# Four-layer graph attention: twelve instead of ten groups of two heads mixed while the adjacency is packed, with three, two or no tiles beside each

## The chip, the cores and the metric

The kernel runs on one core of one Trainium2 chip. The metric is the device time of one execution in microseconds (us); the time quoted for a kernel is the median of its runs. Engines are named as the profile names them: PE is TensorE (PEld its weight loads), DVE is VectorE, ACT is ScalarE, POOL is GpSimd and SP is SyncE, whose queue issues the transfers spoken of here.

## What is computed

Four graph-attention layers over 4096 nodes with 256 features, each followed by a residual sum and a layer norm. The change touches the first layer alone, which has four heads of 64 features:

```python
h = jnp.einsum('nf,hfd->hnd', x, W)
s_src = jnp.einsum('hnd,hd->hn', h, a1)
s_dst = jnp.einsum('hnd,hd->hn', h, a2)
e = jax.nn.leaky_relu(s_src[:, :, None] + s_dst[:, None, :], 0.01)
e = jnp.where(adj[None, :, :] == 0, -jnp.inf, e)
alpha = jax.nn.softmax(e, axis=-1)
out = jnp.einsum('hij,hjd->hid', alpha, h)
```

`adj` is a 4096 x 4096 int32 matrix, 64 MB, and it is used by all four layers. It is read once, at the start, and kept on the chip as one bit per entry.

## The kernel before, in words

**Packing.** The adjacency comes in 32 tiles of 128 rows. A tile is two halves of 1 MB (`load_adj`, L416, on SP's queue). There is room for one tile, one buffer for each half, so the transfer of a half is issued only when DVE has converted the same half of the tile before it. `convert` (L1712, the instruction is L1717) makes a half into bf16; `pack_half` (L1307, L1313) multiplies it on PE by powers of two so that eight entries become one byte; ACT stores the finished tile (`store_packed`, L935, L938). Seven tiles are packed before the attention begins (`PACKED_FIRST`), the other 25 beside its first groups.

**Mixing.** Each head is one pass, and a pass is eight groups of 512 target nodes. A group has eight units; in one unit ACT makes four tiles `above` (L967), DVE makes two masks from them and from the packed bits (L1792, L1797, L1800), and PE multiplies the masks by the head's values: 32 matmuls (L1370, L1373). Two sets of masks are kept, so DVE is at most two units ahead of PE. In the units 1 to 4 of the next group DVE adds up the banks (`sum_parts`, L1951); then POOL divides (`quotient`, L615: five instructions from L626 to L639), and this must have ended two groups later, when DVE wants the same slot of sums (`banks_ready`, L1953). A group needs the four tiles of its own 512 nodes packed.

**The opening.** `FRONT` (L70) lists the groups that run while tiles are still being packed, as pairs of head and group; its places are counted from 0 here. It holds all eight groups of head 0, with two of head 1 between them. Beside the group at place `at` stand the tiles `packs_of(at)`, three for each place until they are used up: three each at places 0 to 7, one at place 8, none at place 9. DVE converts one half in each of the units 0 to 5, right behind the masks of the unit; PE packs a half one unit later; ACT stores a tile behind `above` of units 4 and 6, the third one behind unit 0 of the next group.

**SP's queue.** For each place SP issues the loads of the tiles of the place before it, then waits until ACT has ended `above` of the group before it (`s_above`, L456), then loads the next row of scores (L432), and goes on with the next place. So the first tile of a place is asked for when ACT has ended the last unit of the group ahead of it, behind the row.

**Values of the next heads.** POOL also makes the values of each later head, eight calls of `values_of` (L654) with twelve instructions each (L542 to L556). Those of head 1 are made at places 0 to 2. Those of head 2 take the room of head 0's values, so they wait for the last group of head 0 (L669, `s_unit`), which is place 9, the end of `FRONT`. PE starts the pass of head 2 only when all eight are there (`one_pass`, L1393, `s_vals`). After `FRONT` the six other groups of head 1 follow, which are called places 10 to 15 here; the pass of head 2 begins at place 16. `front` (L660) sets POOL's order: the first values, the quotient of place 9, two more values, and from then on one call of `values_of` and one quotient in turn.

Of the kernel before, what the change touches and what calls it, by code (L numbers as in the profile page):

```python
# [21 lines left out]
T = N // P  # L22
# [10 lines left out]
BITS = 8  # L33
# [33 lines left out]

FRONT = [(0, 0), (0, 1), (0, 2), (0, 3), (1, 0), (0, 4), (0, 5), (0, 6), (1, 1), (0, 7)]  # L70
PACKS = 3


def packed_before(at):

    return min(PACKED_FIRST + at * PACKS, T)


def packs_of(at):

    return range(packed_before(at), packed_before(at + 1))


assert all(packed_before(at) >= (g + 1) * GT for at, (p, g) in enumerate(FRONT))

AHEAD = 3
# [78 lines left out]
def gnn_kernel(nc, A, out, last_layer=3):  # L168

    with ExitStack() as ctx:  # L170
# [406 lines left out]
        def _(pool):  # L577
# [82 lines left out]
            def front():  # L660

                values = {0: (0, 1, 2), 1: (3, 4, 5), 2: (6, 7)}
                for at, (p, g) in enumerate(FRONT[:-1]):
                    for v in values.get(at, ()):
                        values_of(0, 1, v)
                    if at == 0:
                        pool.wait_ge(s_rowexp, 1)
                    quotient(0, p, g, at % 2, at)
                pool.wait_ge(s_unit, len(FRONT) * BITS + CREDIT)  # L669
                values_of(0, 2, 0)  # L670
                quotient(0, *FRONT[-1], 1, len(FRONT) - 1)
                values_of(0, 2, 1)
                values_of(0, 2, 2)
                for g in range(2, NG):
                    if g + 1 < NG:
                        values_of(0, 2, g + 1)
                    quotient(0, 1, g, g % 2)
                chain.settle()
# [179 lines left out]
        def _(act):  # L858
# [68 lines left out]
            def stores_behind(at, par, k):  # L927

                other = GT * (1 - par)
                if k in (4, 6) and k // 2 - 2 < len(packs_of(at)):  # L930
                    store_packed(packs_of(at)[k // 2 - 2], other + k // 2 - 2)
                if k == 0 and at > 0 and len(packs_of(at - 1)) == PACKS:
                    store_packed(packs_of(at - 1)[PACKS - 1], GT * par + PACKS - 1)

# [75 lines left out]
            def attention(l):  # L1010

                act.wait_ge(s_kpass, l * H + 1)
                if l == 0:
                    for at, (p, g) in enumerate(FRONT):
                        group(0, p, None, at % 2, first=(at == 0), at=at)
                        if at == 0:
                            scores_of(0, 1)
                else:
                    for par in range(2):
                        group(l, 0, 0, par, first=(par == 0))  # L1020
                    with act.Fori(1, NG // 2) as gg:
                        for par in range(2):
                            group(l, 0, gg, par)
                for p in range(1, H):
                    if l > 0 or p > 1:
                        scores_of(l, p)
                    if l == 0 and p == H - 1:
                        for g in range(NG):
                            group(l, p, g // 2, g % 2, elu=ELU_AT.get(g))
                        continue  # L1030
                    with act.Fori(1 if l == 0 and p == 1 else 0, NG // 2) as gg:
                        for par in range(2):
                            group(l, p, gg, par)

# [239 lines left out]
        def _(pe):  # L1274
# [81 lines left out]
            def group(l, slot, par, at, packs=(), first=False):  # L1356

                for k in range(BITS):
                    if first and k % 2 == 0:
                        pe.wait_ge(s_vfirst, first_values_before(l) + k + 2)  # L1360
                    pe.wait_ge(s_sides, at * BITS + (TURN[l] * H * UNITS + k + 1 + CREDIT))
                    pe.nop(nofuse=True)
                    for q in range(Q):
                        v = values[:, slot, k * Q + q, :]
                        start, final = (k == 0 and q == 0), (k == BITS - 1 and q == Q - 1)
                        for it in range(GT):
                            acc = bank[GT * par + it]
                            rows = slice(it * P, (it + 1) * P)
                            if l < 3:
                                pe.matmul(acc[:, 0:KW], pos[:, k % 2, q, :].bitcast(FP8)[:, rows], v[:, 0:KW],  # L1370
                                          start=start, stop=final, skip_group_check=True)

                                last = pe.matmul(acc[:, KW:2 * KW], neg[:, k % 2, q, :].bitcast(FP8)[:, rows],  # L1373
                                                 v[:, KW:2 * KW], start=False, stop=final, skip_group_check=True)
                            else:
                                last = pe.matmul(acc[:, 0:2 * KW], edge[:, k % 2, q, :].bitcast(FP8)[:, rows], v,  # L1376
                                                 start=start, stop=final)
                    last.then_inc(s_unit, 1)
                    if 1 <= k <= 2 * len(packs):
                        n, half = divmod(k - 1, 2)  # L1380
                        if half == 0:
                            if at == 0:
                                pe.wait_ge(s_src, 1)
                                pe.wait_ge(s_packed, PACKED_FIRST + CREDIT)
                            else:
                                pe.wait_ge(s_banksum, PACKS * (at - 1) + n + 1)
                        pack_half(packs[n], half, GT * (1 - par) + n)

            def one_pass(l, p):

                begun = p == 0 or (l == 0 and p == 1)
                if p > 0:
                    pe.wait_ge(s_vals, p * NG + values_before(l))  # L1393
                if p == 0:
# [1 line left out]
                        pe.wait_ge(s_sums, TURN[l] * SUMS + par + 1)  # L1396
                        group(l, 0, par, par, first=(par == 0))
                final = l == 3 and p == PASSES[3] - 1
                with pe.Fori(1 if begun else 0, NG // 2 - final) as gg:
                    for par in range(2):  # L1400

                        pe.wait_ge(s_sums, gg * 2 + (p * NG + TURN[l] * SUMS + par + 1))
                        pe.nop(nofuse=True)
                        group(l, p % 2, par, gg * 2 + (p * NG + par))
# [275 lines left out]
        def _(dve):  # L1680
# [313 lines left out]
            def group(l, g, gg, par, banks_before, norm=None, first=False, front=None, fold=None, ahead=None,  # L1994
# [7 lines left out]
                for k in range(BITS):  # L2002
# [53 lines left out]
                    if front is not None:  # L2056
                        if l == 0 and first and k == 0:
                            store_packed(PACKED_WOVEN + 1, 6 + (PACKED_WOVEN + 1) % 2)
                        if k < 2 * len(packs_of(g)):
                            convert(packs_of(g)[k // 2], k % 2)  # L2060
                    if fold is not None and k >= GT:
                        fold_weights(fold, k - GT)
                    if norm is not None:
# [17 lines left out]
            def attention(l):  # L2081
                if l == 0:
                    for at, (p, g) in enumerate(FRONT):
                        group(0, at, None, at % 2, 1 - at % 2 if at else None, first=(at == 0), front=g,
                              fold=1 if at == len(FRONT) - 1 else None)
                    one_pass(0, 1, 1)
                    one_pass(0, 2)
                    final_pass(0)
                    return
# [365 lines left out]
```

## Time and profile before

| | |
|---|---|
| median of 3 runs | 3026.6 us (3025.57 to 3028.38) |
| span of the profiled execution | 3025.2 us |
| PE busy | 2947.3 us, 97% of the span |
| DVE, ACT, POOL busy | 2138.8, 1921.5, 1173.2 us |
| HBM read | 97.73 MB, of which `adj` is 64 transfers of 1024 KB |

The span runs from the first to the last instruction of the profiled execution; it lies 1.4 us under the median of the runs. Idle time of PE counts directly, since PE is the engine that is busy nearly all the time; idle time of the others counts only where PE waits for them. A line such as L1370 is a line of the kernel before. Matmuls overlap, so their single durations (246 ns) are longer than the step from one to the next.

### The profile page before, as it was taken

To read this page: it belongs to the slowest core of one execution; us is meant where nothing else is said; L and a number is where in the kernel's file an instruction comes from. 1 tells how busy PE (TensorE), PEld (TensorE's weight loads), DVE (VectorE), ACT (ScalarE), POOL (GpSimd) and SP (SyncE) were. 2 spreads that over 40 slices of the span, in tenths; PEclk is the share of its full clock that TensorE was granted. 3 is DMA by queue.
4 is the path that set the end of the run, shared out by engine and by line. 5 is a ranking of instruction groups with operands and counts; after the bars stand their busy time and mean duration, and the time that the engine had idled before them with its cause. 6 is when DMAs were issued, how large, how long until landed. Compare 5 with 4: busy or idle time off the path is not lost.

```text
span 3025.2 us, 65221 instructions
## 1 busy us (share of the span) xinstructions
PE 2947.3 (97%) x24628; PEld 2580.8 (85%) x24628; DVE 2138.8 (71%) x3855; ACT 1921.5 (64%) x3414; POOL 1173.2 (39%) x1559
## 2 busy tenths in 40 slices
PE   7899999999989999999999999999999999989999
PEld 6899999999989999999998877888788878755555
DVE  5998888888988888888886556665666666562245
ACT  4777899999988999999995544454455444430000
POOL 0661385642226656564222023233333333444222
PEclk9999999999999999999999999999999999999999
DMA  8667100000100000000010000000000000000001
GB/s 289 203 206 246 60 15 11 14 11 15 61 12 15 11 11 14 11 14 11 15 34 12 4 1 4 4 1 4 1 4 4 1 1 1 2 1 1 0 14 42
DMA packets 41912, 104.55 MB, mean 35 GB/s; under 512 B 9856, under 2 KB 23424, under 8 KB 33536
## 3 DMA queue, kind: packets, MB, share of 16 engines
q1 hardware_dynamic: 39616, 101.61, 10.3%
q8 instruction: 111, 1.82, 0.2%
q10 hardware_dynamic: 2112, 0.52, 0.1%
q14 instruction: 73, 0.60, 0.1%
HBM read 97.73 MB, written 4.39 MB: 34 GB/s over the span
## 4 chain that ended last, share of the span: by engine, by line
PE 88%; DVE 5%; DMA 3%; ACT 2%; issue 2%; POOL 1%; SPq 0%; DVEq 0%; POOLq 0%; ACTq 0%
PE bank L1373 21%; PE bank L1370 21%; PE bank L1428 15%; PE bank L1466 13%; PE bank L1376 11%; DMA arena<-in_adj_dram 3%; PE bank L1301 2%; PE bank L1455 2%; PE bank L1442 1%; DVE rings L1797 1%; DVE arena L1717 1%; ACT above L967 1%; PE bank L1313 1%; PE bank L1351 1%; DVE rings L1792 1%
## 5 line engine op out<-in xcount | busy, mean ns | idle before, releaser
L1370 PE MATMUL bank<-values,rings 128*128 128x195 bf16 x8192 | 1413.3, 246 | 35.9 <-DVE rings L1800 24.0
L1373 PE MATMUL bank<-values,rings 128*128 128x195 bf16 x8192 | 1413.4, 249 | 0.0
L967 ACT ACTIVATE above<-srow,kpass 128x512 fp8e4<-128x512 f32 x2032 | 1280.1, 709 | 121.3 <-DVE rings L1800 114.6
L1370 PEld LDWEIGHTS bank<-values,rings 128*128 128x128 fp8e4 x8192 | 806.1, 98 | 45.1 <-issue 43.1
L1373 PEld LDWEIGHTS bank<-values,rings 128*128 128x128 fp8e4 x8192 | 788.7, 96 | 0.4
L1797 DVE TENSOR_TENSOR rings<-rings,above 128x512 uint32<-128x512 uint32 x512 | 399.6, 781 | 184.6 <-PE bank L1373 160.9
L1055 ACT ACTIVATE values<-srow,cmul 128x512 f32<-128x512 f32 x256 | 205.8, 814 | 411.2 <-PE bank L1466 410.3
L1800 DVE TENSOR_TENSOR rings<-rings 128x512 uint32<-128x512 uint32 x512 | 430.6, 841 | 17.3
L1466 PE MATMUL bank<-hv,values 128*128 128x257 f32 x1792 | 420.6, 380 | 0.0
L1466 PEld LDWEIGHTS bank<-hv,values 128*128 128x128 f32 x1792 | 335.0, 190 | 69.9 <-issue 25.2
L1376 PE MATMUL bank<-values,rings 128*128 128x390 bf16 x1920 | 320.4, 329 | 11.5 <-DVE values L1833 11.5
L1376 PEld LDWEIGHTS bank<-values,rings 128*128 128x128 fp8e4 x1920 | 186.8, 97 | 145.1 <-issue 14.5
L626 POOL TENSOR_TENSOR quot<-sums,cmul 128x260 f32<-128x260 f32 x64 | 50.3, 786 | 597.8 <-DVE sums L1951 475.9
L1792 DVE TENSOR_SCALAR rings<-packed 128x512 uint32 (+1 forms) x512 | 242.4, 474 | 5.8 <-ACT packed L938 5.7
L1907 DVE SCALAR_TENSOR_TENSOR values<-values,cmul,rings 128x512 f32<-128x512 f32 x256 | 192.0, 757 | 35.0 <-ACT values L1055 34.3
L759 POOL TENSOR_SCALAR zrow<-zrow 128x1 f32<-128x1 f32 x128 | 46.2, 361 | 429.4 <-DVE zrow L2159 429.3
L2022 DVE TENSOR_SCALAR rings<-packed 128x512 uint32 (+1 forms) x120 | 54.7, 456 | 201.0 <-PE bank L1376 200.9
L1951 DVE TENSOR_REDUCE sums<-bank 128x130 f32<-128x390 f32 x320 | 176.6, 554 | 3.7 <-PE bank L1351 2.0
L1428 PE MATMUL bank<-arena,above 128*128 128x256 f32 (+1 forms) x496 | 165.9, 482 | 0.8 <-ACT above L1110 0.8
L1428 PEld LDWEIGHTS bank<-arena,above 128*128 128x128 f32 x496 | 94.0, 190 | 53.1 <-issue 43.8
L1428 PE MATMUL bank<-quot,arena 128*128 128x256 f32 x512 | 118.3, 379 | 0.0
L762 POOL TENSOR_TENSOR zrow<-zrow,exponents 128x1 f32<-128x1 f32 x128 | 103.6, 809 | 19.6 <-POOL zrow L759 0.6
(223 smaller groups left out, 3482.9 us busy)
## 6 DMA issues: line engine op xcount, KB each, us to landing
arena<-in_adj_dram SPq DMA_DIRECT2D x64, 1024.0 KB, 5.0
srow<-src_dram SPq DMA_DIRECT2D x69, 256.0 KB, 3.1
x<-in_x_dram SPq DMA_DIRECT2D x4, 1024.0 KB, 11.4
out_dram<-x SPq DMA_DIRECT2D x7, 512.0 KB, 2.9
arena<-in_L_gnn_fe_w_dram SPq DMA_DIRECT2D x2, 512.0 KB, 6.9
arena<-in_L_gnn_W_hz_dram SPq DMA_DIRECT2D x1, 1024.0 KB, 7.6
arena<-in_L_gnn_g_w_dram SPq DMA_DIRECT2D x1, 1024.0 KB, 10.9
weights<-in_L_gnn_W_dram SPq DMA_DIRECT2D x3, 256.0 KB, 4.0
```

The source lines that it names most:

```text
L967: last = act.activation(above[:, k % 2, q, :], srow[:, par, :], ACT.Relu, scale=BIG, bias=kpass[:, p % 2, k * Q + q:k * Q + q + 1], satura ...
L1055: act.activation(w2[:, m % DEPTH, :], srow[:, g % 2, :], ACT.Relu, scale=b_col[:, jt:jt + 1], bias=c_neg[:, jt:jt + 1]).then_inc(E.relu, 1)
L1370: pe.matmul(acc[:, 0:KW], pos[:, k % 2, q, :].bitcast(FP8)[:, rows], v[:, 0:KW], start=start, stop=final, skip_group_check=True)
L1373: last = pe.matmul(acc[:, KW:2 * KW], neg[:, k % 2, q, :].bitcast(FP8)[:, rows], v[:, KW:2 * KW], start=False, stop=final, skip_group_chec ...
L1376: last = pe.matmul(acc[:, 0:2 * KW], edge[:, k % 2, q, :].bitcast(FP8)[:, rows], v, start=start, stop=final)
L1428: last = pe.matmul(dst, lhsT[k], rhs[k], start=(k == 0), stop=(k == len(lhsT) - 1))
L1466: last = pe.matmul(bank[it][:, 0:VW], w2[:, m % DEPTH, it * P:(it + 1) * P], hv[:, k * Q + q, :], start=(k == 0 and q == 0), stop=False)
L1792: dve.tensor_scalar(edge[:, r], words, shift[0], ONE, shift[1], ALU.bitwise_and).then_inc(s_dve, 1)
L1797: dve.tensor_tensor(pos[:, r], edge[:, r], above[:, r].bitcast(U32), ALU.bitwise_and).then_inc(s_dve, 1)
L1800: dve.tensor_tensor(neg[:, r], edge[:, r], pos[:, r], ALU.bitwise_xor).then_inc(s_sides, 1)
L1907: dve.scalar_tensor_tensor(out=w2[:, m % DEPTH, :], in0=w2[:, m % DEPTH, :], scalar=c_pos[:, jt:jt + 1], in1=edge[:, unit % 2, q, :].bitca ...
L1951: return dve.tensor_reduce(sums[:, slot, it, :, :], parts, AX.X, ALU.add)
```

## The change

Head 1 has four groups in the opening instead of two, so `FRONT` has twelve places. The last group of head 0 stands at place 10, and the last place, 11, is a group of head 1. The tiles beside the places are listed in a table: three at places 0 to 4 as before, then two at places 5 to 9, none at places 10 and 11. Where two tiles stand beside a group, DVE converts halves in units 0, 1, 3 and 4, and ACT stores them behind units 4 and 7. On POOL the first values of head 2 wait for place 10, then comes the quotient of place 11, then four calls of `values_of` in a row (`BEGUN` is 4) instead of two, then the turns from group 4 on. The loops over the rest of head 1 begin at group 4.

```diff
-FRONT = [(0, 0), (0, 1), (0, 2), (0, 3), (1, 0), (0, 4), (0, 5), (0, 6), (1, 1), (0, 7)]
+FRONT = [(0, 0), (0, 1), (0, 2), (0, 3), (1, 0), (0, 4), (1, 1), (0, 5), (1, 2), (0, 6), (0, 7), (1, 3)]
 PACKS = 3
+GROUP_PACKS = (3, 3, 3, 3, 3, 2, 2, 2, 2, 2, 0, 0)
+HALF_AT = {3: {0: (0, 0), 1: (0, 1), 2: (1, 0), 3: (1, 1), 4: (2, 0), 5: (2, 1)},
+           2: {0: (0, 0), 1: (0, 1), 3: (1, 0), 4: (1, 1)}, 0: {}}
+STORE_AT = {3: {4: 0, 6: 1}, 2: {4: 0, 7: 1}, 0: {}}
 def packed_before(at):
-    return min(PACKED_FIRST + at * PACKS, T)
+    return PACKED_FIRST + sum(GROUP_PACKS[:at])
+BEGUN = len(FRONT) - NG
...
-                pool.wait_ge(s_unit, len(FRONT) * BITS + CREDIT)
+                pool.wait_ge(s_unit, (FRONT.index((0, NG - 1)) + 1) * BITS + CREDIT)
                 values_of(0, 2, 0)
                 quotient(0, *FRONT[-1], 1, len(FRONT) - 1)
-                values_of(0, 2, 1)
-                values_of(0, 2, 2)
-                for g in range(2, NG):
+                for v in range(1, BEGUN + 1):
+                    values_of(0, 2, v)
+                for g in range(BEGUN, NG):
                     if g + 1 < NG:
                         values_of(0, 2, g + 1)
                     quotient(0, 1, g, g % 2)
...
-                if k in (4, 6) and k // 2 - 2 < len(packs_of(at)):
-                    store_packed(packs_of(at)[k // 2 - 2], other + k // 2 - 2)
+                if k in STORE_AT[GROUP_PACKS[at]]:
+                    n = STORE_AT[GROUP_PACKS[at]][k]
+                    store_packed(packs_of(at)[n], other + n)
...
-                    if 1 <= k <= 2 * len(packs):
-                        n, half = divmod(k - 1, 2)
+                    if k - 1 in HALF_AT[len(packs)]:
+                        n, half = HALF_AT[len(packs)][k - 1]
...
-                        if k < 2 * len(packs_of(g)):
-                            convert(packs_of(g)[k // 2], k % 2)
+                        if k in HALF_AT[GROUP_PACKS[g]]:
+                            n, half = HALF_AT[GROUP_PACKS[g]][k]
+                            convert(packs_of(g)[n], half)
```

Lines of the changed kernel are about ten higher from `front` on. On DVE at place 5 (its second and third unit; L1717, after the change L1728, converts a half, L1951 or L1962 sums a bank, the other lines make masks), before:

```order
L1717 TENSOR_SCALAR arena<-arena 128x2048 [waits pack_matmul,adj_loaded1]
L1792 TENSOR_SCALAR rings<-packed 128x512
L1797 TENSOR_TENSOR rings<-rings,above 128x512 [waits unit_multiplied,above_made,dve_chain]
L1800 TENSOR_TENSOR rings<-rings 128x512 [waits dve_chain]
L1951 TENSOR_REDUCE sums<-bank 128x130
L1717 TENSOR_SCALAR arena<-arena 128x2048 [waits pack_matmul,adj_loaded0]
```

and after:

```order
L1728 TENSOR_SCALAR arena<-arena 128x2048 [waits pack_matmul,adj_loaded1]
L1803 TENSOR_SCALAR rings<-packed 128x512
L1808 TENSOR_TENSOR rings<-rings,above 128x512 [waits unit_multiplied,above_made,dve_chain]
L1811 TENSOR_TENSOR rings<-rings 128x512 [waits dve_chain]
L1962 TENSOR_REDUCE sums<-bank 128x130
L1803 TENSOR_SCALAR rings<-packed 128x512
```

Behind the third unit no half is converted any more; the next one stands behind the fourth unit. The first conversion of the group, behind its first unit, keeps its place.

On POOL, behind the quotient of the last place of `FRONT` and the next three sets of values (L542 to L556, after the change L552 to L566), before:

```order
L553 CAST values<-vtmp_pool 128x4x65 [waits pool_chain]
L556 TENSOR_TENSOR values<-vtmp_pool,values 128x4x65 [waits pool_chain]
L626 TENSOR_TENSOR quot<-sums,cmul 128x260 [waits quotients_made,sums_made]
L627 TENSOR_TENSOR quot<-sums,cmul 128x260
L631 TENSOR_TENSOR quot<-quot 128x260 [waits pool_chain]
L635 TENSOR_TENSOR quot<-quot,exponents 128x4 [waits pool_chain]
```

and after:

```order
L563 CAST values<-vtmp_pool 128x4x65 [waits pool_chain]
L566 TENSOR_TENSOR values<-vtmp_pool,values 128x4x65 [waits pool_chain]
L552 COPY vtmp_pool<-emul 128x4
L553 TENSOR_TENSOR vtmp_pool<-hv,emul 128x4x64
L557 CAST values<-vtmp_pool 128x4x65 [waits pool_chain]
L560 TENSOR_TENSOR vtmp_pool<-vtmp_pool,values 128x260 [waits pool_chain]
```

Where a quotient (L626 and on) stood, a fourth set of values follows, and a fifth behind it; the next quotient, that of place 12, stands behind both.

## Rows read from the trace of the kernel before

**Rows 1.** The page: busy us of each engine, and the chain that ended last.

```profile
PE 2947.3 (97%) x24628; PEld 2580.8 (85%) x24628; DVE 2138.8 (71%) x3855; ACT 1921.5 (64%) x3414; POOL 1173.2 (39%) x1559
PE 88%; DVE 5%; DMA 3%; ACT 2%; issue 2%; POOL 1%; SPq 0%; DVEq 0%; POOLq 0%; ACTq 0%
```

**Rows 2.** PE's waits from 60 to 700 us: in all, times, longest.

```profile
PE bank L1370 <- DVE rings L1800: 17.7, 21, 2.3
```

**Rows 3.** Stretches: length, busy us (instructions) of PE, PEld, DVE, ACT, POOL, then PEclk.

```profile
204.10:231.47 27.37, 27.37 (x355) 27.28 (x353) 23.47 (x34) 21.60 (x36) 5.45 (x5) 1.00 0.67 225
231.47:259.86 28.39, 27.58 (x354) 27.23 (x353) 24.01 (x34) 21.70 (x36) 5.45 (x5) 1.00 0.71 231
259.86:289.47 29.61, 27.74 (x354) 27.19 (x353) 24.09 (x34) 21.93 (x36) 5.45 (x5) 1.00 0.68 225
289.47:317.79 28.32, 27.58 (x352) 27.24 (x353) 25.47 (x36) 21.47 (x36) 5.46 (x5) 1.00 0.80 268
317.79:363.66 45.87, 45.87 (x546) 45.50 (x545) 36.58 (x65) 41.37 (x67) 9.18 (x10) 1.00 0.05 17
407.45:495.13 87.68, 87.68 (x1026) 87.48 (x1025) 75.64 (x113) 81.12 (x130) 55.61 (x74) 1.00 0.04 12
```

**Rows 4.** PE in order of time: start, us, instruction [idle before it <- releaser].

```profile
256.23 1.05 PE L1313 MATMUL bank<-powers,arena 128*128 128x128 bf16 x16
257.12 0.25 PE L1370 MATMUL bank<-values,rings 128*128 128x195 bf16 x1
...
264.52 0.24 PE L1370 MATMUL bank<-values,rings 128*128 128x195 bf16 x1 [1.76 <-DVE rings L1800]
```

**Rows 5.** DVE in order of time, around the first conversions at places 5, 6, 7.

```profile
231.97 1.23 DVE L1717 TENSOR_SCALAR arena<-arena 128x2048 bf16<-128x2048 int32 x1 [2.42 <-DMA arena<-in_adj_dram]
...
261.36 1.23 DVE L1717 TENSOR_SCALAR arena<-arena 128x2048 bf16<-128x2048 int32 x1 [3.41 <-DMA arena<-in_adj_dram]
...
289.91 1.23 DVE L1717 TENSOR_SCALAR arena<-arena 128x2048 bf16<-128x2048 int32 x1 [0.69 <-DMA arena<-in_adj_dram]
```

**Rows 6.** SP's queue in order of time: the rows of scores ahead of each tile.

```profile
224.62 0.33 SPq L432 DMA_DIRECT2D srow<-src_dram  x1
...
252.92 0.33 SPq L432 DMA_DIRECT2D srow<-src_dram  x1
...
282.31 0.33 SPq L432 DMA_DIRECT2D srow<-src_dram  x1
```

**Rows 7.** ACT in order of time at place 5, units 4 to 6.

```profile
242.59 0.60 ACT L938 ACTIVATE packed<-bank 128x512 uint8<-128x512 f32 x1 [1.55 <-PE bank L1313]
243.09 5.00 ACT L967 ACTIVATE above<-srow,kpass 128x512 fp8e4<-128x512 f32 x8
```

**Rows 8.** POOL in order of time: first and last instructions of values and quotients.

```profile
379.68 0.38 POOL L542 COPY vtmp_pool<-emul 128x4 f32<-128x4 f32 x1
...
408.00 1.07 POOL L626 TENSOR_TENSOR quot<-sums,cmul 128x260 f32<-128x260 f32 x1
...
413.16 0.39 POOL L542 COPY vtmp_pool<-emul 128x4 f32<-128x4 f32 x1
...
422.13 1.07 POOL L626 TENSOR_TENSOR quot<-sums,cmul 128x260 f32<-128x260 f32 x1
...
474.83 0.92 POOL L556 TENSOR_TENSOR values<-vtmp_pool,values 128x260 bf16<-128x260 f32 x1
...
487.72 0.67 POOL L639 TENSOR_TENSOR hv<-quot 128x256 f32<-128x256 f32 x1
```

**Rows 9.** Two stretches behind an idle PE; columns as in the stretches above.

```profile
91.95:95.36 3.41, 3.41 (x23) 3.17 (x22) 3.34 (x5) 2.24 (x4) 0.00 (x0) 0.50 0.00 0
887.25:894.08 6.83, 4.05 (x26) 3.74 (x27) 5.67 (x11) 6.67 (x12) 1.96 (x3) 0.50 0.53 116
```

**Rows 10.** PE in order of time: what it waited for before those two.

```profile
91.70 0.24 PE L1370 MATMUL bank<-values,rings 128*128 128x195 bf16 x1 [2.29 <-DVE rings L1800]
...
890.03 0.32 PE L1370 MATMUL bank<-values,rings 128*128 128x195 bf16 x1 [5.73 <-DVE values L1833]
```

More of the change, by code:

```diff
@@ L65 @@
 TURN = {0: 0, 1: 1, 3: 2}
-FRONT = [(0, 0), (0, 1), (0, 2), (0, 3), (1, 0), (0, 4), (0, 5), (0, 6), (1, 1), (0, 7)]
+FRONT = [(0, 0), (0, 1), (0, 2), (0, 3), (1, 0), (0, 4), (1, 1), (0, 5), (1, 2), (0, 6), (0, 7), (1, 3)]
 PACKS = 3
+GROUP_PACKS = (3, 3, 3, 3, 3, 2, 2, 2, 2, 2, 0, 0)
+HALF_AT = {3: {0: (0, 0), 1: (0, 1), 2: (1, 0), 3: (1, 1), 4: (2, 0), 5: (2, 1)},
+           2: {0: (0, 0), 1: (0, 1), 3: (1, 0), 4: (1, 1)}, 0: {}}
+STORE_AT = {3: {4: 0, 6: 1}, 2: {4: 0, 7: 1}, 0: {}}
 def packed_before(at):
-    return min(PACKED_FIRST + at * PACKS, T)
+    return PACKED_FIRST + sum(GROUP_PACKS[:at])
 def packs_of(at):
     return range(packed_before(at), packed_before(at + 1))
+assert packed_before(len(FRONT)) == T and sum(p for p, g in FRONT) == FRONT[-1][1] + 1
 assert all(packed_before(at) >= (g + 1) * GT for at, (p, g) in enumerate(FRONT))
+BEGUN = len(FRONT) - NG
 AHEAD = 3
@@ L1030, in attention @@
                         continue
-                    with act.Fori(1 if l == 0 and p == 1 else 0, NG // 2) as gg:
+                    with act.Fori(BEGUN // 2 if l == 0 and p == 1 else 0, NG // 2) as gg:
                         for par in range(2):
@@ L1389, in one_pass @@
             def one_pass(l, p):
-                begun = p == 0 or (l == 0 and p == 1)
+                begun = 1 if p == 0 else BEGUN // 2 if (l, p) == (0, 1) else 0
                 if p > 0:
@@ L1398, in one_pass @@
                 final = l == 3 and p == PASSES[3] - 1
-                with pe.Fori(1 if begun else 0, NG // 2 - final) as gg:
+                with pe.Fori(begun, NG // 2 - final) as gg:
                     for par in range(2):
@@ L2085, in attention @@
                               fold=1 if at == len(FRONT) - 1 else None)
-                    one_pass(0, 1, 1)
+                    one_pass(0, 1, BEGUN // 2)
                     one_pass(0, 2)
```

## The prediction

> **What bounds the kernel now.** I read the page first: PE is busy 97% of the span and holds 88% of the chain that ended last [rows 1], so only what moves PE moves the time. Then PE's waits in the first 700 us: masks of DVE that came late cost it 17.7 us in 21 waits, the longest 2.3 us [rows 2]. Places 0 to 4 of the opening stay as they are, so the question is how much of this lies from place 5 on. The stretches are cut at the first matmul of a group: place 4, 5, 6, 7, then places 8 and 9 together, then places 12 to 15 [rows 3]. Four groups without packing take 87.68 us, 21.92 each, or 2.74 per unit. A packed half is worth the step from its first matmul to the next unit's, 257.12 - 256.23 = 0.89 us [rows 4]. Three tiles make a group 21.92 + 6 x 0.89 = 27.26 us. Place 4 took 27.37, which is PE's own pace. Places 5, 6 and 7 took 28.39, 29.61 and 28.32, so 1.13, 2.35 and 1.06 too much, and places 8 and 9 took 45.87 against 2 x 21.92 + 2 x 0.89 = 45.62, so 0.25 too much [rows 3]. In all 4.79 us: more than that the opening from place 5 on can't give.
>
> Where it comes from is seen at place 6. PE stood idle for 1.76 us before its second unit, waiting for DVE [rows 4]; DVE itself had stood idle for 3.41 us before its first conversion, waiting for the adjacency [rows 5]. That half was asked for right behind the row of scores, when ACT had ended the group before: the row was issued at 252.92 and the conversion began at 261.36, a lag of 8.44 us; at places 5 and 7 it was 7.35 and 7.60 [rows 5, 6]. From the start of the conversion to PE's second unit it took 264.52 - 261.36 = 3.16 us, and that unit was due 2.74 us behind the start of the group. So PE is late by (issue of the row - start of the group) + lag + 0.42. With -6.85, -6.94 and -7.16 us in the bracket, this gives 0.92, 1.92 and 0.86 us at places 5, 6 and 7, 3.70 of the 4.79.
>
> **The change part by part.** *What PE computes* is the same: the same groups, the same 25 tiles, and a group of head 1 costs PE what one of head 0 costs. Nothing is removed; work moves.
>
> *Two tiles instead of three.* PE needs 21.92 + 4 x 0.89 = 25.48 us for such a group. The first conversion still stands behind the first unit, and its transfer is still asked for when ACT has ended the group before. So the bracket decides. In a group of two tiles ACT stores the first tile behind unit 4, and must wait for PE to pack its second half, as it waited 1.55 us for it in the group before the change [rows 7]. PE ends that half 2.74 + 2 x 3.63 = 10.00 us into the group; the store takes 0.50 (243.09 - 242.59), and three more units of `above` follow at about 2.45 us, half of the 5.00 us that eight of its instructions took, less their overlap [rows 7]. This is 17.9 us, with some 0.3 us for the hand-overs 18.2, and the group ends at 25.48: a bracket of -7.25, hardly better than -6.94. Behind such a group PE is late by 0.52, 0.77 or 1.61 us for the lags 7.35, 7.60 and 8.44. I take 7.60, the middle one. Place 5 follows a group of three tiles as before and keeps its 0.92; places 6 to 9 make 4 x 0.77 = 3.1; the 0.25 at the end, where DVE also folds weights, moves to place 11. In all 4.3 against 4.79: a gain of 0.5, between a gain of 1.5 and a loss of 2.9. The rest of DVE's excess goes, since units without a conversion leave it room.
>
> *The other order of the groups.* Place 10 needs all 32 tiles. The last is packed 20.0 us into place 9 and stored by ACT right behind its last unit; DVE needs it for the first masks of place 10, which can't be finished before PE has ended unit 6 of place 9, at 22.7. The store has 2 us of cover, so I count nothing.
>
> *POOL, the values of head 2.* Here the change has a price. The first set waits for place 10 and is hidden in places 11 and 12. Then the order has the quotient of place 11, whose sums DVE makes only in place 12. A quotient of this kind ended at 487.72 + 0.67 = 488.39, and the group before which its sums were made began at 495.13 - 21.92 = 473.21 [rows 3, 8]: 15.2 us into the group. Seven sets are queued behind it, and two quotients among them, those of places 12 and 13. Three sets in a row took 408.00 - 379.68 = 28.32, so 9.44 each; one behind a quotient took 422.13 - 413.16 = 8.97; a quotient took 413.16 - 408.00 = 5.16 [rows 8]. Five sets at 9.44, two at 8.97 and two quotients are 75.5 us, and the last set is there 90.7 us behind the start of place 12. The pass of head 2 is due after four groups, at 87.7. PE waits 3.0 us; with all sets at 8.97 it is 0.6, with all at 9.44 it is 3.9. Before the change the last set ended at 474.83 + 0.92 = 475.75, some 19 us ahead of the pass at 495.13 [rows 3, 8]; two places are lost to it, 43.8 us, and only part comes back by making sets closer together. The quotient of place 12 ends about 67.5 us behind the start of place 12, and DVE wants it at 65.8 + 2: just in time.
>
> *The clock.* After an idle time of 2.29 us PE's granted clock was 0.50 (1.2 GHz) for 3.41 us, and 23 PE instructions ran where 3.41 / 2.74 x 32 = 40 fit at the full clock: 17 lost, 1.4 us. After 5.73 us idle it was 0.50 for 6.83 us, of which PE worked 4.05, so 2.0 us lost [rows 9, 10]. After the 1.76 us at place 6 the clock stayed at 1.00 [rows 3, 4]. A wait of 3.0 us is nearest to the first: 1.4 us, between nothing and 2.0. The Trainium skill, "TensorE: Matmul & The Clock Gate", section "Terms", prices such a stretch at its whole length times the withheld share of the clock. By this the two stretches would cost 1.7 and 3.4 us; the sum would come to +4.2 or +5.9 instead of +3.9. The rows disagree for the longer one, since PE was idle in part of it anyway.
>
> The sum: -0.5 + 3.0 + 1.4 = +3.9 us. The profiled execution becomes 3025.2 + 3.9 = 3029.1, and with the 1.4 us by which the median of the runs lies above it, 3030.5.
>
> **The rivals.** *The values come in time.* If POOL makes each set in 8.97 us, PE waits 0.6 us and the clock holds: -0.5 + 0.6 = +0.1, 3026.7 us. For it speaks that sets behind a quotient were that short; against it that five of seven stand behind another set.
>
> *The transfers come in time.* If the lag at places 6 to 9 is 6.8 us or less, their 3.1 us go too: +0.8, 3027.4 us. DVE's evener work speaks for it; against it, that the three lags in the rows were all over 7.3 and that nothing in the change issues these transfers earlier against the end of the group.
>
> *The transfers come late, and the kernel is slower.* If each of the four lags is like the 8.44 at place 6, the loss of 2.9 takes the place of the gain: 2.9 + 3.0 + 1.4 = +7.3, 3033.9 us. There are now four such starts behind two-tile groups where there were two late ones, and each pays. It decides from a mean lag of about 8.2, where the sum passes 6.05 us.
>
> *The change does not do what it says.* It can't reach a gain of 6 us: all that is late from place 5 on is 4.79.
>
> **How the numbers follow.** 0.2% of 3026.6 is 6.05 us, about what a measurement of this kernel can tell from no change. The forecast, a late head 2 and a small gain in the opening (3028 to 3032.5), gets 0.60; values in time 0.15; transfers in time 0.07; transfers late 0.17; a gain over 6 us 0.01. So faster 0.01, same 0.82, slower 0.17. The range, 3026.5 to 3034.0, holds the forecast, the case of early transfers, half of the case of values in time and most of the late transfers.
>
> **What would show it.** Right: places 6 to 9 of about 26.2 us each, with DVE idle before the first conversion of each; POOL without a pause from some 15 us into place 12 until the last set; PE idle for about 3 us before the first matmul of place 16, waiting for POOL's `values`, and a stretch at 0.50 behind it. Wrong: places 6 to 9 at 25.5 us, or 27; no idle PE before place 16; or a wait at place 10 or 15 that I counted at nothing.

## The result, and the profile after

The changed kernel took 3036.99 us, the median of six runs (3033.65 to 3041.35). The kernel before took 3027.49 us in six runs beside them. The ratio is 1.0033, with a 95% interval from 1.0023 to 1.0043: a loss of 9.5 us. It is outside the range of the prediction, which ended at 3034.0. The profiled execution took 3038.3 us with a span of 3036.2, so the two profiles differ by 11.0 us of span. The parts below are those of these two profiles.

On the page, the busy time of each engine and the chain that ended last (as [rows 1]):

```profile
PE 2952.6 (97%) x24628; PEld 2584.7 (85%) x24628; DVE 2138.2 (70%) x3855; ACT 1920.3 (63%) x3414; POOL 1173.3 (39%) x1559
...
PE 83%; DVE 6%; POOL 3%; DMA 3%; issue 2%; ACT 2%; SPq 0%; POOLq 0%; DVEq 0%; ACTq 0%
```

PE holds 83% of the chain where it held 88%; DVE gained one point and POOL two. PE is busy 5.3 us longer with the same 24628 instructions. A slower clock does this: where its granted clock was 0.50 a matmul took 0.37 us (at 319.73), and at 1.00 it took 0.25, all of it counted as busy. Three such stretches are not in the profile before. One, in place 0, cost one unit 1.6 us and was made good by a shorter wait in place 1; the other two are at places 8 and 16, below.

The stretches from place 5 on, cut at the first matmul of each group (as [rows 3]: length, busy us (instructions) of PE, PEld, DVE, ACT, POOL, then PEclk). They are places 5, 6, 7, 8, 9, 10, 11, then 12 to 15 together, then place 16, the first group of head 2:

```profile
231.52:258.18 26.66, 25.63 (x323) 25.43 (x322) 21.83 (x32) 21.41 (x35) 5.15 (x5) 1.00 0.47 167
258.18:285.10 26.92, 25.64 (x323) 25.43 (x322) 21.83 (x32) 21.12 (x35) 5.15 (x5) 1.00 0.49 169
285.10:311.82 26.72, 25.62 (x322) 25.41 (x321) 21.83 (x32) 21.10 (x35) 5.15 (x5) 1.00 0.47 163
311.82:341.14 29.32, 27.27 (x323) 26.79 (x322) 21.69 (x32) 21.02 (x35) 5.15 (x5) 0.94 0.49 168
341.14:367.32 26.18, 25.62 (x322) 25.41 (x321) 22.26 (x33) 21.11 (x35) 5.15 (x5) 1.00 0.36 121
367.32:389.22 21.90, 21.90 (x259) 21.90 (x258) 16.77 (x28) 20.61 (x35) 4.19 (x5) 1.00 0.08 22
389.22:412.25 23.03, 22.50 (x259) 21.71 (x258) 20.49 (x36) 19.78 (x33) 11.24 (x15) 1.00 0.06 13
412.25:504.10 91.85, 87.81 (x1025) 87.38 (x1025) 80.95 (x117) 85.32 (x137) 73.76 (x104) 0.99 0.04 12
504.10:528.29 24.19, 24.19 (x257) 23.84 (x257) 16.07 (x24) 16.07 (x26) 13.11 (x20) 0.90 0.04 13
```

Place 5 begins at 231.52 where it began at 231.47, so everything lies behind it. With place 16 the stretch was 285.56 us long before and is 296.77 now. The difference of 11.2 us by its parts, each beside the prediction's term:

| part | before | after | difference | forecast |
|---|---|---|---|---|
| places 5 to 11 | 175.98 | 180.73 | +4.7 | -0.5 |
| places 12 to 15 | 87.68 | 91.85 | +4.2 | +3.0 |
| place 16 | 21.90 | 24.19 | +2.3 | +1.4 |

Every term is above its forecast, and the first one has the other sign.

**Places 5 to 9** took 135.80 us, where five groups at PE's own pace of 25.48 would take 127.40: 8.4 too much. Before, the same five places took 132.19, 4.8 too much. Taken from the steps between PE's units, the second unit is late by 1.19, 1.44, 1.26, 2.21 and 0.72 us, in all 6.8; the other 1.6 is one unit of place 8 at a slower clock. SP's queue in order of time, the rows of scores for places 6, 8 and 9 (as [rows 6]):

```profile
251.58 0.33 SPq L442 DMA_DIRECT2D srow<-src_dram  x1
...
305.50 0.33 SPq L442 DMA_DIRECT2D srow<-src_dram  x1
...
333.83 0.33 SPq L442 DMA_DIRECT2D srow<-src_dram  x1
```

Against the starts 258.18, 311.82 and 341.14 the bracket (issue of the row minus start of the group) is -6.60, -6.32 and -7.31; at place 7, whose row was issued at 278.48, it is -6.62. The forecast had -7.25 for all four. DVE in order of time, its first conversions at places 6 and 8 (as [rows 5]):

```profile
259.20 1.23 DVE L1728 TENSOR_SCALAR arena<-arena 128x2048 bf16<-128x2048 int32 x1 [1.75 <-DMA arena<-in_adj_dram]
...
313.62 1.23 DVE L1728 TENSOR_SCALAR arena<-arena 128x2048 bf16<-128x2048 int32 x1 [2.52 <-DMA arena<-in_adj_dram]
```

The lags are 259.20 - 251.58 = 7.62 and 313.62 - 305.50 = 8.12. DVE still stands idle for the transfer before each of these.

**Why the row goes out later** is seen in place 5. First DVE's masks of units 4 and 5, then ACT's `above`, then POOL's quotient, each in order of time:

```profile
242.48 0.42 DVE L1803 TENSOR_SCALAR rings<-packed 128x512 uint32<-128x512 uint32 x1
242.94 0.69 DVE L1808 TENSOR_TENSOR rings<-rings,above 128x512 uint32<-128x512 uint32 x1
243.66 0.69 DVE L1811 TENSOR_TENSOR rings<-rings 128x512 uint32<-128x512 uint32 x1
...
245.88 0.85 DVE L1803 TENSOR_SCALAR rings<-packed 128x512 uint32<-128x512 uint32 x1
246.76 0.99 DVE L1808 TENSOR_TENSOR rings<-rings,above 128x512 uint32<-128x512 uint32 x1
247.79 1.11 DVE L1811 TENSOR_TENSOR rings<-rings 128x512 uint32<-128x512 uint32 x1
```

```profile
243.40 5.00 ACT L978 ACTIVATE above<-srow,kpass 128x512 fp8e4<-128x512 f32 x8
248.99 2.56 ACT L978 ACTIVATE above<-srow,kpass 128x512 fp8e4<-128x512 f32 x4 [0.60 <-DVE rings L1811]
```

```profile
244.96 1.48 POOL L636 TENSOR_TENSOR quot<-sums,cmul 128x260 f32<-128x260 f32 x1 [21.64 <-DVE sums L1962]
...
249.92 0.62 POOL L649 TENSOR_TENSOR hv<-quot 128x256 f32<-128x256 f32 x1
```

While the quotient runs, from 244.96 to 250.54, the three mask instructions of one unit take 2.95 us together instead of 1.80, and those of the next 2.19. ACT has run ahead here, since its second store now stands behind the last unit and no longer behind unit 6, and its last four tiles of `above` wait 0.60 us until DVE has ended these masks. The row for place 6 waits for that ACT work, and is issued at 251.58 right behind it (248.99 + 2.56 = 251.55).

**PE's waits** at place 8 and before place 16, in order of time (as [rows 10]), and the two stretches in which its granted clock was 0.50 (as [rows 9]):

```profile
316.77 0.24 PE L1381 MATMUL bank<-values,rings 128*128 128x195 bf16 x1 [2.06 <-DVE rings L1811]
...
504.10 0.32 PE L1381 MATMUL bank<-values,rings 128*128 128x195 bf16 x1 [4.04 <-POOL values L566]
```

```profile
317.80:321.20 3.40, 3.40 (x24) 3.12 (x23) 2.96 (x6) 2.56 (x5) 0.00 (x0) 0.50 0.95 311
502.20:509.00 6.80, 4.90 (x31) 4.58 (x32) 0.27 (x1) 2.38 (x4) 4.62 (x7) 0.50 0.01 2
```

The first is the lateness of place 8. Behind it PE worked at 0.50, its lower level of 1.2 GHz, for 3.4 us. The second is the wait for head 2's values.

**POOL** around that wait (as [rows 8]): the quotient of place 11, the first instruction of the next set, and the last of the last set:

```profile
422.77 0.68 POOL L636 TENSOR_TENSOR quot<-sums,cmul 128x260 f32<-128x260 f32 x1 [8.46 <-issue]
...
427.37 0.65 POOL L552 COPY vtmp_pool<-emul 128x4 f32<-128x4 f32 x1
...
502.88 0.66 POOL L566 TENSOR_TENSOR values<-vtmp_pool,values 128x260 bf16<-128x260 f32 x1
```

POOL stands idle for 8.46 us with seven sets queued behind the quotient. It ends the quotient 427.37 - 412.25 = 15.1 us into place 12, and the last set 503.54 - 412.25 = 91.3 us behind the start of place 12.

**Place 11** took 23.03 us. There DVE folds weights, and POOL makes the quotient of place 10 and then the first set of head 2 beside it. DVE in order of time, masks of one unit:

```profile
400.76 0.99 DVE L1808 TENSOR_TENSOR rings<-rings,above 128x512 uint32<-128x512 uint32 x1
401.79 1.11 DVE L1811 TENSOR_TENSOR rings<-rings 128x512 uint32<-128x512 uint32 x1
```

They are as slow as those beside the quotient of place 5. PE's last four units of the group took 2.89, 2.88, 3.00 and 3.32 us. At place 9 of the kernel before, where DVE folded beside a quotient and POOL made no set, they took 2.89, 2.88, 2.74 and 2.74.

### The profile page after: what moved, and what is told of

The parts are those of the page before. It is cut to its first block, busy times and chain, and to the rows that moved or that the text cites. A ratio compares the mean times of both kernels' runs of the same rounds, so it can differ in the third digit from the quotient of the medians.

```text
span 3036.2 us, 65123 instructions
## 1 busy us (share of the span) xinstructions
PE 2952.6 (97%) x24628; PEld 2584.7 (85%) x24628; DVE 2138.2 (70%) x3855; ACT 1920.3 (63%) x3414; POOL 1173.3 (39%) x1559
## 4 chain that ended last, share of the span: by engine, by line
PE 83%; DVE 6%; POOL 3%; DMA 3%; issue 2%; ACT 2%; SPq 0%; POOLq 0%; DVEq 0%; ACTq 0%
PE bank L1384 19%; PE bank L1381 19%; PE bank L1439 15%; PE bank L1477 13%; PE bank L1387 11%; DMA arena<-in_adj_dram 3%; PE bank L1312 2%; PE bank L1466 2%; DVE rings L1808 1%; PE bank L1453 1%; ACT above L978 1%; DVE arena L1728 1%; DVE rings L1803 1%; PE bank L1362 1%; DVE rings L1811 1%
## 5 line engine op out<-in xcount | busy, mean ns | idle before, releaser
L1808 DVE TENSOR_TENSOR rings<-rings,above 128x512 uint32<-128x512 uint32 x512 | 396.6, 775 | 197.5 <-PE bank L1384 165.6
L636 POOL TENSOR_TENSOR quot<-sums,cmul 128x260 f32<-128x260 f32 x64 | 51.6, 806 | 616.1 <-DVE sums L1962 505.5
L1803 DVE TENSOR_SCALAR rings<-packed 128x512 uint32 (+1 forms) x512 | 242.0, 473 | 2.6 <-ACT packed L949 2.4
L1962 DVE TENSOR_REDUCE sums<-bank 128x130 f32<-128x390 f32 x320 | 176.5, 554 | 3.8 <-PE bank L1362 2.0
```

Source lines behind the costliest of these rows:

```text
L1803: dve.tensor_scalar(edge[:, r], words, shift[0], ONE, shift[1], ALU.bitwise_and).then_inc(s_dve, 1)
L1808: dve.tensor_tensor(pos[:, r], edge[:, r], above[:, r].bitcast(U32), ALU.bitwise_and).then_inc(s_dve, 1)
L1962: return dve.tensor_reduce(sums[:, slot, it, :, :], parts, AX.X, ALU.add)
```

## The experiments

Three parts could be told apart: the transfers of places 5 to 9, the values of head 2, and the clock behind its wait. pool_set_ahead, three_tiles, tile_ahead and set_and_tile_ahead ran on one chip, where the kernel before took 3027.11 us (32 runs); the other four on another, where it took 3026.8 (26 runs). In profiles of kernels that do the same up to there, place 5 begins anywhere from 231.2 to 235.0 us. So the stretches from place 5 on are the finer measure, and medians carry that scatter too.

**pool_set_ahead**: one set of head 2 goes ahead of the quotient of place 11.

```diff
+                values_of(0, 2, 1)
                 quotient(0, *FRONT[-1], 1, len(FRONT) - 1)
-                for v in range(1, BEGUN + 1):
+                for v in range(2, BEGUN + 1):
```

> The changed kernel with one edit on POOL: the second set of head 2's values stands ahead of the quotient of place 11 instead of behind it, in the time in which POOL stood still for 8.46 us. Theory (the late values cost their wait and the slow clock behind it): the first set ended about 2 us into place 12, the second then ends at about 11.6, the quotient at 17, and behind it stand six sets and two quotients instead of seven and two, so the last set is there about 83.5 us behind the start of place 12, 4 us ahead of the pass. PE's idle 4.04 us before place 16 and the 2.30 us in place 16 go: 3036.99 - 6.5 = about 3030.5 us. Rival (POOL's wait only hides another one, of DVE's masks or ACT): place 15 stays at about 26 us and the time at 3037.

It took 3032.92 us, 1.0019 (1.001 to 1.0028) of the kernel before. Its stretches for places 11, 12, 13 to 15, and 16:

```profile
387.69:410.72 23.03, 22.50 (x259) 21.71 (x257) 20.49 (x36) 19.78 (x33) 11.24 (x15) 1.00 0.04 13
410.72:433.17 22.45, 22.28 (x256) 21.72 (x257) 20.59 (x29) 20.63 (x33) 19.70 (x28) 1.00 0.04 14
433.17:498.85 65.68, 65.68 (x770) 65.67 (x769) 59.41 (x84) 61.19 (x98) 58.28 (x78) 1.00 0.05 13
498.85:520.75 21.90, 21.90 (x259) 21.90 (x258) 18.63 (x29) 20.14 (x33) 12.31 (x18) 1.00 0.04 14
```

The wait before place 16 is gone, and so is the slow clock behind it. Places 11 to 16 took 133.06 us instead of 139.07: 6.0 back; the median is 4.1 us lower than that of the changed kernel. So the wait came from the order on POOL, the quotient ahead of the sets, and not from an engine that had no time left. The price is 0.5 us at place 12, which DVE enters late from the fold and where it now works beside a set in the idle time POOL had. In set_tile_ahead_fold, below, the set stands there too but the fold does not come just before it, and the 0.5 is gone.

**pe_kept_busy**: ahead of PE's wait for these values, 48 matmuls into a bank that is free; what they write is overwritten.

```diff
+            FILL = 48
+            fill = powers[:, :, :].rearrange("p k n -> p (k n)")[:, 0:KW]
...
+                if (l, p) == (0, 2):
+                    pe.wait_ge(s_sums, p * NG + 1)
+                    for _ in range(FILL):
+                        pe.matmul(bank[0][:, 0:KW], powers[:, 0, :], fill, start=True, stop=True)
```

> The changed kernel with 48 matmuls of 195 columns into a bank that is free, put ahead of PE's wait for the values of head 2; their results are overwritten, they only keep PE busy for about 4 us of the wait. Theory (the first unit of place 16 took 5.04 us instead of 2.74 because PE had stood idle before it and its clock was halved): place 15 still ends 4 us late, since POOL is as late as before, but place 16 takes 21.9 us instead of 24.2: 3037 - 2.3 = about 3034.7 us. Rival (the long first unit is DVE's or ACT's lateness after the wait): place 16 stays at 24 us.

It took 3035.9 us, 1.0029 (1.0017 to 1.004). Its stretches for places 15 and 16:

```profile
479.39:505.49 26.10, 26.10 (x306) 25.90 (x305) 22.16 (x32) 24.51 (x41) 23.02 (x33) 1.00 0.03 11
505.49:527.39 21.90, 21.90 (x256) 21.90 (x257) 16.29 (x24) 16.01 (x26) 13.10 (x20) 1.00 0.04 14
```

Place 15 is as long as before, since the values are no earlier. Place 16 takes 21.90 us instead of 24.19. The 2.3 us are shown to be the clock alone: what PE waits for is unchanged, and only its idle time was filled. The median moved by 1.1 us, less than the stretch did; the intervals of the two kernels overlap.

**three_tiles**: the twelve groups stay, but tiles stand beside them three at a time as long as there are any; the two tables of units get an entry for one tile.

```diff
-GROUP_PACKS = (3, 3, 3, 3, 3, 2, 2, 2, 2, 2, 0, 0)
+GROUP_PACKS = (3, 3, 3, 3, 3, 3, 3, 3, 1, 0, 0, 0)
```

> The changed kernel with the packing table undone: three tiles beside places 0 to 7 and one beside place 8, as before the change; the twelve groups and POOL's order stay. Theory (values late 4.2, clock 2.3, folding beside POOL's first set 1.1, the two-tile places 3.6): the 3.6 go and the rest stays, place 10 begins at about 363.7 as before the change, place 15 still takes 26 us, and the time is about 3027.5 + 7.6 = 3035. Rival (the spread of the tiles is the whole loss): 3028.

It took 3035.66 us, 1.0025 (1.0015 to 1.0034). Places 5 to 9 took 367.22 - 235.01 = 132.21 us, 3.6 less than in the changed kernel. Against the profiles of pool_set_ahead and pe_kept_busy, where these places have the changed spread too and took 134.56 and 135.52, it is 2.4 and 3.3 less. So the more even spread costs 2.4 to 3.6 us here. That the kernel before had 132.19 is in part chance, since the parts differ: the second units are late by 2.2 us in all instead of 3.7, and a later half of place 6 by 1.3. The wait before place 16 (4.04 us) and the 23.02 us of place 11 stayed, which ties them to the twelve groups and not to the spread. The median is only 1.3 us lower than the changed kernel's. In this profile place 5 began 3.5 us later; whether it did so in the other runs is not known.

**tile_ahead**: SP asks for the first tile of a place before it waits for ACT, ahead of the row of scores.

```diff
-                        for t in (*packs_of(at - 1), *(packs_of(at) if at == len(FRONT) - 2 else ())):
+                        ahead = len(FRONT) if at == len(FRONT) - 2 else at
+                        for t in range(packed_before(at - 1) + 1, min(packed_before(ahead) + 1, T)):
```

> The changed kernel with one edit on SP's queue: the first tile of the next place is asked for ahead of the wait for ACT and of the row of scores, as soon as its buffers are converted. Theory (PE is late at each place because this transfer is asked for when ACT has ended the group before): DVE no longer waits before the first conversion, places 5 to 9 take 25.5 us each instead of 26.2 to 29.3, which is 8 us, and places 1, 2 and 4 gain 1 to 2 us more; values and clock stay as they are. 3037 - 9.5 = about 3027.5 us. Rival (the transfers are bound by bandwidth, not by when they are asked for): places 5 to 9 stay at 26 to 27 us, and the time at 3036 or more.

It took 3027.75 us, 1.0002 (0.9993 to 1.0011). SP's queue ahead of place 5, and the stretches of places 5 and 6:

```profile
218.73 0.33 SPq L431 DMA_DIRECT2D arena<-in_adj_dram  x1
220.53 0.33 SPq L442 DMA_DIRECT2D srow<-src_dram  x1
```

```profile
227.71:253.18 25.47, 25.47 (x323) 25.47 (x322) 21.01 (x31) 21.29 (x35) 5.15 (x5) 1.00 0.53 177
253.18:278.65 25.47, 25.47 (x323) 25.47 (x322) 21.74 (x33) 20.99 (x35) 5.15 (x5) 1.00 0.54 176
```

The half is asked for 9.0 us ahead of the start of the place instead of behind the row, and PE does not wait any more: places 5 to 9 took 127.34 us, which is PE's own pace, and no slow clock followed. So all 8.4 us of excess, the slow clock at place 8 included, came from the transfer being asked for too late. Places 1 to 4 also fell, from 120.87 to 118.88 us.

**set_and_tile_ahead**: both edits together.

> The changed kernel with both edits: the second set of values ahead of the quotient of place 11, and the first tile of the next place asked for ahead of the row. Theory (the two losses are apart from each other and add up): 3037 - 6.5 - 9.5 = about 3021 us, under the kernel before. Rival (one hides the other, so that only the larger goes): 3027.

It took 3021.89 us, 0.998 (0.9971 to 0.9989). Places 5 to 9 took 127.35 us, places 15 and 16 21.89 each. In the stretches the two edits add up: 8.5 us from places 5 to 9 and 6.0 from places 11 to 16, as each gave alone, and 2.2 from places 1 to 4. The medians agree less well: against the changed kernel both edits together gave 15.1 us, where alone they gave 9.2 and 4.1.

**quotient_later**: POOL's quotients of places 4 to 8, which run beside places 5 to 9, wait until ACT has ended the `above` of the group beside them. Nothing else is moved.

```diff
+                    if 4 <= at <= 8:
+                        pool.wait_ge(s_above, (at + 2) * BITS)
```

> The changed kernel with one more wait on POOL: the quotients of places 4 to 8 start when ACT has ended `above` of the place behind, instead of in the middle of it. Theory (in a two-tile place POOL's quotient runs beside DVE's unit 5, makes its masks slow, so that ACT ends the place, and the first transfer of the next place is asked for, 0.6 us later than the prediction had it): ACT ends about 7.2 us ahead of the end of the place instead of 6.3 to 6.6, PE's second unit is late by 0.6 to 0.7 us at places 6 to 8 instead of 1.3 to 2.2, the slow clock at place 8 stays away; places 5 to 9 take 131.5 to 133 us instead of 135.8, so 3037 - 3.5 = about 3033.5 us. Rival (it is ACT's wait for the packed tile alone that decides, and the quotient is hidden): places 5 to 9 stay at 135 to 136 us.

It took 3035.55 us, 1.003 (1.0018 to 1.0041). The rows of scores for places 6 and 7, then the stretches of places 6 to 8:

```profile
251.73 0.33 SPq L442 DMA_DIRECT2D srow<-src_dram  x1
...
277.66 0.33 SPq L442 DMA_DIRECT2D srow<-src_dram  x1
```

```profile
259.04:284.97 25.93, 25.63 (x322) 25.43 (x321) 20.72 (x33) 21.01 (x35) 4.14 (x5) 1.00 0.52 173
284.97:310.84 25.87, 25.63 (x323) 25.42 (x321) 20.69 (x32) 21.00 (x35) 4.14 (x5) 1.00 0.50 175
310.84:338.04 27.20, 25.63 (x323) 25.43 (x321) 20.70 (x32) 21.01 (x35) 4.14 (x5) 1.00 0.46 164
```

The bracket is 251.73 - 259.04 = -7.31 at place 6, 277.66 - 284.97 = -7.31 at place 7, and -7.31 again at places 8 and 9. DVE is busy 20.7 us in a place instead of 21.8: 1.1 us of its time were the quotient's doing. Places 5 to 9 took 131.56 us instead of 135.80 (134.56 and 135.52 in pool_set_ahead and pe_kept_busy). Of the 4.2 us, 1.6 is the slow clock of place 8, which didn't come behind an idle time of 1.57 us. The second units were late by 0.86, 0.46, 0.40, 1.72 and 0.76 us, 4.2 in all instead of 6.8. The median is only 1.4 us below the changed kernel's and their intervals overlap, so what is shown is the bracket and the stretch, not a gain in the total.

**before_tile_ahead**: the kernel before with SP's edit of tile_ahead alone.

> The kernel before, with the one edit on SP's queue: the first tile of the next place asked for ahead of the row. Theory (what the opening loses from place 5 on is the late transfer, with three tiles as with two): places 5 to 7 take 27.3 us each instead of 28.4, 29.6 and 28.3, places 1, 2 and 4 gain up to 3 us; 3027.1 - 4.5 - 1.5 = about 3021 us, no slower than the version of the change with both edits (3021.9). Rival (with three tiles DVE has no room, so the wait for the transfer only turns into DVE's own time): 3025 to 3027.

It took 3020.66 us, 0.9978 (0.997 to 0.9987). The stretches of places 5 and 7, then of 8 and 9 together:

```profile
228.94:256.19 27.25, 27.25 (x354) 27.25 (x353) 23.91 (x34) 21.48 (x36) 5.45 (x5) 1.00 0.73 242
...
283.68:311.21 27.53, 27.48 (x352) 27.22 (x353) 25.12 (x36) 21.47 (x36) 5.45 (x5) 1.00 0.77 253
311.21:357.08 45.87, 45.87 (x546) 45.50 (x545) 36.59 (x65) 41.39 (x67) 9.18 (x10) 1.00 0.07 17
```

Three tiles beside a group fit: places 5 to 9 took 128.14 us against PE's 127.40. DVE has the time for them; what was late was the request.

**set_tile_ahead_fold**: set_and_tile_ahead with the fold of weights at place 10 instead of 11.

```diff
-                              fold=1 if at == len(FRONT) - 1 else None)
+                              fold=1 if at == len(FRONT) - 2 else None)
```

> The changed kernel with both edits (second set ahead of the quotient, first tile ahead of the row) and a third: DVE folds the next layer's weights at place 10 instead of place 11. Theory (at place 11 the folding meets POOL's first set, and DVE's masks come late; at place 10 it meets only a quotient): place 11 takes 21.9 us instead of 23.0, place 10 takes 22.2 instead of 21.9, so about 0.8 us less than without it: 3021.9 - 0.8 = 3021 us, to be read in the profile rather than in the median. Rival (the folding isn't what slows place 11): place 11 stays at 23 us.

It took 3020.6 us, 0.998 (0.9972 to 0.9989). Its stretches for places 10 and 11:

```profile
355.29:377.47 22.18, 22.18 (x258) 21.81 (x257) 19.68 (x36) 20.64 (x34) 5.05 (x5) 1.00 0.08 22
377.47:399.37 21.90, 21.90 (x258) 21.90 (x257) 18.23 (x28) 20.16 (x33) 10.10 (x15) 1.00 0.04 13
```

Place 11 is back at PE's pace, and place 10 has the 0.3 us that the fold costs where POOL makes no set beside it. With the 0.5 us that went at place 12 too, the fold beside a set of POOL was worth 1.4 us in the stretches; in the medians 1.3, inside the scatter.

The two fastest versions, the kernel before with an earlier request and the twelve groups with three repairs, can't be told apart. Twelve groups and two tiles show no gain of their own.

## Why the prediction was wrong, and where it was right

**The step that failed is the bracket of a two-tile group, -7.25.** It was built from PE's packing and ACT's store and three units of `above`: 18.2 us from the start of the group to the next row, if nothing else is late. That sum was right in itself. In quotient_later the row is issued 19.02 us into place 5 (251.73 - 232.71), and that place was 0.86 us over PE's 25.47, which leaves 18.16; the next three places give 18.16 too. With it the five second units were late by 4.2 us, where the forecast had 4.0. It left out that ACT, with no store between unit 4 and the last unit, comes up against DVE, whose masks POOL's quotient slows at just that time. The 0.7 us that this costs at places 5 and 6 and the 1.0 at place 7 (18.87, 18.85 and 19.15 in the same working) go whole into the lateness of the next group. Before the change the quotient slowed the masks alike (0.85, 1.00 and 1.11 us in place 5), but there ACT stood waiting for PE at that time. ACT in order of time, the kernel before, its store behind unit 6:

```profile
249.85 0.60 ACT L938 ACTIVATE packed<-bank 128x512 uint8<-128x512 f32 x1 [1.77 <-PE bank L1313]
```

So the wait for PE's packing set the measured -6.94, and slow masks could add to it only through PE, whose fifth unit took 3.84 us instead of 3.63. My sum took this wait away and did not ask which wait comes next. Only at place 8 did the row come by the sum, -7.31 ahead of place 9: that group was so late that ACT waited 3.18 us for PE's packing (at 325.86) and then ran its last twelve tiles of `above` in a row without a wait.

| lateness at places 5 to 9 | forecast | measured | of it bracket | of it lag |
|---|---|---|---|---|
| sum, us | 4.0 | 6.8 | +2.1 | +0.7 |

The lag was taken at 7.60 and came out at 7.46 to 7.63 but for one, the 8.12 at place 8. The same place 8 was late again in pool_set_ahead (an idle time of 2.23 us), pe_kept_busy (2.47) and quotient_later (1.57), so it belongs to the program and not to chance. The traces have a candidate for its cause: a read of 16 KB on the queue that the page calls instruction, while the half is on its way. From the changed kernel's DMA queues, 305 to 315 us:

```profile
q8 instruction: 1, 0.02, 0.6%
```

It starts at 309.25, which is 3.75 us behind the row, and takes 0.95 us. In the profiles of the two kernels and of pool_set_ahead, pe_kept_busy, three_tiles and quotient_later such a read starts 3.2 to 4.5 us behind a row of places 1 to 9 nine times, also at place 6 of the kernel before. Each time DVE's conversion begins 4.34 to 4.38 us behind the start of the read, with a lag of 7.56 to 8.81. Later reads left a mark in some places (5.40 and 6.54 us behind the row at place 8 of pe_kept_busy and quotient_later, lags 8.52 and 8.61) and none in others (6.33 at place 6 of the changed kernel, 7.62). No run took a read away, so the cause is not shown.

**A second slow clock was not foreseen.** I let a wait of 1.76 us pass without a price, since the clock held behind it in the kernel before. At place 8 the idle time was 2.06 us, and 1.6 us more were lost behind it. The rival of late transfers had the right sign and the right place, but its +2.9 (2.8 by its own terms) had no term for the clock either, and the long lag that it put at all four places came at one.

**The fold** was moved to place 11 at its old price of 0.25 us. It costs 1.1 there, since POOL makes the first set of head 2 beside it. "Moves" was the wrong word for a step whose neighbours change. Lateness 2.8 and clock 1.6 and fold 0.85 are 5.2 us, which is where +4.7 instead of -0.5 comes from.

**The values of head 2** were right as a mechanism: the quotient of place 11 ended 15.1 us into place 12 (forecast 15.2), the last set 91.3 behind its start (90.7), and PE stood idle. The sizes were off by 1.2 us: 0.6 in POOL's work, and 0.56 from the end of POOL's last instruction, 503.54, to PE's first matmul, 504.10, which I had not counted. The sum also has an error of its own. Three of the seven sets stand behind a quotient and not two, which would make 90.2 by its prices. But these three took 9.25, 9.70 and 9.11 us and the other four 9.15 to 9.59, so the single 8.97 in [rows 8] was no price for a set behind a quotient, and the rival of values in time, which rested on it, lost its ground.

**The clock at place 16** came as forecast, at 2.3 us instead of 1.4. The wait of 4.0 us came with a slow stretch of 6.8 us, like the one in [rows 9] that lost 2.0 us, while I had taken the shorter one as nearest. The Trainium skill, "TensorE: Matmul & The Clock Gate", section "Terms", prices it at 6.8 x 0.5 = 3.4. The trace disagrees as it did before, since PE was idle in 1.9 us of the stretch. For place 8, where PE worked throughout, the same price gives 1.7 beside a measured 1.6, and there the trace agrees.

**Counted at nothing, and rightly:** place 10 behind the last store took 21.90 us, and places 13 and 14 are PE's pace, so the quotient of place 12 was in time.

The range failed because each bound took its unknown alone. The opening's bounds had the lags in them, but not the bracket, which I held to be worked out.

## What to carry to other kernels

When an engine is relieved so that another can run ahead, look at what the second one meets next, and with whose durations it was last measured: a sum of undisturbed steps must be checked against the rows in which a third engine runs beside them. A transfer that waits in an in-order queue behind a wait for something it doesn't need is worth moving first; here that one edit gave 6.1 us in the kernel before and 9.2 in the changed one, and the evener spread of the work gave nothing. When work is queued behind an instruction that waits, count what it is due for from there to the end, with the hand-over.

## What the hardware showed beyond that

**DVE beside POOL.** In places 5 and 11 of the changed kernel two-input masks of 128 x 512 took 0.69 us alone and 0.77 to 1.11 beside most instructions of POOL's quotient or its sets, and the instruction ahead of them, L1803, up to 0.85 instead of 0.42. Beside the quotient's L645, which works on 128 x 4 values, nothing was lost: in place 5 L1803 took 0.41 at 248.82 and L1808 0.69 at 249.27. POOL can lose too: L636 took 1.48 us beside a conversion of DVE (at 244.96) and 0.68 at 422.77. The Trainium skill, "SBUF — State Buffer", section "Terms", says that VectorE and GpSimd share a pair of ports to which one of them has sole right while its instruction lasts. The direction agrees with the trace; that DVE stood still for a whole instruction of POOL can't be read from it, since one of the masks lost up to 0.4 us where POOL's instructions last 0.6 to 1.5, and none beside the 1.29 of L645.

**The length of an idle time did not decide the clock.** At place 8 of the changed kernel the clock was 0.50 soon after an idle time of 2.06 us, and in its place 0 after one of 1.93 (at 102.66). In pe_kept_busy PE was idle for 2.83 us early in the opening, and the clock stayed at 1.00 for the next 6.9 us. PE in order of time, and the stretch behind it:

```profile
115.09 0.24 PE L1381 MATMUL bank<-values,rings 128*128 128x195 bf16 x1 [2.83 <-DVE rings L1818]
```

```profile
115.09:122.00 6.91, 6.22 (x77) 6.08 (x78) 6.81 (x9) 5.00 (x8) 5.84 (x8) 1.00 0.69 243
```

So a wait of about 2 to 3 us is to be priced both ways here: at nothing, and at 1.4 to 1.6 us.
